# A gated feed-forward and long-convolution kernel: new instruction orders in its opening, and four of its dequantisation units moved

## The reference

```python
xn = layernorm(x)                        # x: 4 x 512 tokens, 512 features, float32
# S4 part: a causal convolution along the feature axis with one kernel K of 512 taps
K = s4_kernel(Lambda, p, q, Vc @ B, Ct, exp(log_step), 512)
y = irfft(rfft(xn, 1024) * rfft(K, 1024))[..., :512] + D * xn
# feed-forward part: weights are 4-bit codes, a 16-entry table (NF4) times one scale per 64 values
Wg, Wu = dequant(gate_q, gate_absmax), dequant(up_q, up_absmax)    # 1792 x 512
Wd = dequant(down_q, down_absmax)                                  # 512 x 1792
h = silu(xn @ Wg.T) * (xn @ Wu.T)
out = x + y + h @ Wd.T
```

## Time and profile before

| | |
|---|---|
| median of 3 runs | 459.49 us (458.85 to 459.49) |
| profiled execution | 460.08 us, span 458.3 us |
| TensorE busy | 438.2 us, 96% of the span |
| VectorE busy | 398.4 us, 87% |
| ScalarE busy | 278.8 us, 61% |
| GpSimd busy | 214.6 us, 47% |
| mean granted TensorE clock | 0.996 |

### The profile page before, as it was taken

How to read it: one execution, slowest core, us unless ns; L and a number is a source line. 1 busy time by engine, 2 the same in 40 slices (tenths; PEclk the granted TensorE clock), 3 DMA queues, 4 the chain that set the end, 5 groups by cost and what they waited for, 6 DMA issues and landing times.

```text
span 458.3 us, 7272 instructions
## 1 busy us (share of the span) xinstructions
PE 438.2 (96%) x2560; PEld 248.8 (54%) x2560; DVE 398.4 (87%) x641; ACT 278.8 (61%) x472; POOL 214.6 (47%) x163
## 2 busy tenths in 40 slices
PE   1879999999999999999999999999999999999997
PEld 1534444443444444434444444466544788888886
DVE  5988979969889798999897879879996999999993
ACT  7868594295877759588684787856032542445340
POOL 2777299547456848669646847778100000000000
PEclk9989999999999999999999999999999999999999
DMA  8543636022315415155222233457691021101111
GB/s 291 172 131 139 144 75 182 1 92 71 138 47 183 161 47 200 54 183 191 63 69 65 61 80 101 111 187 249 193 369 60 1 94 47 46 1 48 47 47 46
DMA packets 34168, 51.41 MB, mean 112 GB/s; under 512 B 13076, under 2 KB 14164, under 8 KB 33364
## 3 DMA queue, kind: packets, MB, share of 16 engines
q1 hardware_dynamic: 34132, 50.95, 35.3%
HBM read 38.03 MB, written 10.81 MB: 107 GB/s over the span
## 4 chain that ended last, share of the span: by engine, by line
PE 85%; DVE 6%; ACT 2%; issue 2%; DMA 2%; POOL 1%; SPq 0%; DVEq 0%; ACTq 0%; POOLq 0%
PE bank L2264 33%; PE bank L2391 21%; PE bank L2109 16%; PE bank L2341 8%; PE bank L2331 6%; ACT work L936 1%; DMA h<-in_x 1%; DVE h L1438 1%; DVE work L1313 1%; DMA work<-in_q_gate 1%; DVE w L1323 1%; DVE work L1309 1%; PE bank L2145 0%; DVE h L1412 0%; POOL h L845 0%
## 5 line engine op out<-in xcount | busy, mean ns | idle before, releaser
L936 ACT ACTIVATE work<-work 128x512 f32<-128x512 f32 (+1 forms) x234 | 130.0, 628 | 11.5 <-POOL work L845 7.8
L845 POOL TENSOR_SCALAR work<-work 128x512 f32<-128x512 int32 x39 | 85.9, 2202 | 64.4 <-DVE work L1309 46.1
L2264 PE MATMUL bank<-h 128*128 128x512 f16 x360 | 81.5, 379 | 0.9 <-ACT bank L1029 0.9
L2109 PE MATMUL bank<-xT,w 128*128 128x512 f16 (+1 forms) x300 | 66.2, 377 | 2.3 <-DVE w L1323 1.1
L2264 PEld LDWEIGHTS bank<-h 128*128 128x128 f16 x360 | 34.9, 98 | 44.0 <-ACT bank L1029 2.4
L2391 PE MATMUL bank<-wd,work 128*128 128x256 f16 x504 | 56.2, 273 | 0.0
L2264 PE MATMUL bank<-xT,w 128*128 128x512 f16 x240 | 55.4, 379 | 0.0
L2391 PEld LDWEIGHTS bank<-wd,work 128*128 128x128 f16 (+1 forms) x504 | 49.3, 98 | 6.0
L2109 PEld LDWEIGHTS bank<-xT,w 128*128 128x128 f16 x300 | 29.4, 99 | 36.8 <-DVE w L1323 2.4
L1250 ACT ACTIVATE work<-h 128x896 f16<-128x896 f32 x30 | 27.9, 942 | 28.4 <-DVE h L2017 18.3
L2391 PE MATMUL bank<-h,work 128*128 128x256 f16 x378 | 42.2, 273 | 0.0
(11 more groups left out here) (181 smaller groups left out, 672.0 us busy)
## 6 DMA issues: line engine op xcount, KB each, us to landing
moved<-h SPq DMA_DIRECT2D x6, 1024.0 KB, 4.9
h<-moved SPq DMA_DIRECT2D x4, 1536.0 KB, 15.5
h<-in_x SPq DMA_DIRECT2D x8, 512.0 KB, 5.4
xT<-in_x SPq DMA_DIRECT2D x16, 256.0 KB, 3.5
out<-xT SPq DMA_DIRECT2D x15, 256.0 KB, 2.1
work<-in_q_gate SPq DMA_DIRECT2D x14, 256.0 KB, 3.6
work<-in_q_up SPq DMA_DIRECT2D x14, 256.0 KB, 2.9
work<-in_am_gate SPq DMA_DIRECT2D x28, 128.0 KB, 3.1
```

What stands on the lines that cost most here:

```text
L845: pool.tensor_scalar(chain_room(u, "r"), qs[:, u % 2, :], RIGHT_FROM, RIGHT_FROM, ALU.max, ALU.subtract).then_inc(first_done, 1)
L936: nc.scalar.activation(room, qs[:, u % 2, :] if j == 0 else room, KNEE, scale=scale, bias=bias, alpha=below).then_inc(knee_done, 1)
L2109: mm = nc.tensor.matmul(out_b, weights(k)[:, unit, wl, f, :], xT[:, TPC * c + first:TPC * c + last, xl, f, :], start=(i == 0), stop=(i == ...
L2264: mm = nc.tensor.matmul(out_b, weight(wl, f), token(xl, f), start=(n == 0 and i in (1, 5)), stop=(n == 5), skip_group_check=i not in (1, 5))
```

## The change

- SyncE: x tiles 4 and 5 are loaded behind the scales of unit 0 and the codes of unit 2, tiles 6 and 7 behind the scales of unit 1.
- Norms: ScalarE makes those of tiles 0, 1 and 4 (before: 0), GpSimd those of the others. A norm on ScalarE waits for its own chunk's `rstd`.
- VectorE's opening: `scales` between the `rstd(0, i)`, the steps of unit 0 behind them; `stats(4)` later; units 2 and 3 relative to `rstd(1, i)` in a new order, `weight_lo(2)` ahead of it.
- TensorE's opening: 8 and 4 `warm_up` matmuls instead of 10 and 6; `products(1, (0,))` ahead of `turn(4)`.
- GpSimd: the 14 `v_step` move behind `first_pass(8)`.
- In window 3 VectorE makes `weight_lo` of unit 9 ahead of both steps of unit 10 (`LO_SOONER`).
- From window 6 on, the `h_mul(n)` behind two slots of dequantisation comes behind one.
- `EARLY_IN` is (7, 9, 11, 12). Window 8 has places 20 and 21, window 12 places 30, 31 and 32, and `LINE_AT` is 31; places from 33 on are as before.

```diff
@@
-EARLY_IN = (7, 8, 9, 11)
+EARLY_IN = (7, 9, 11, 12)
 EARLY = len(EARLY_IN)
@@
         SUMMED = (1,)
-        POOL_NORMS = 1
+        ACT_NORMS = (0, 1, 4)
+        LO_SOONER = made_before(3) + 1
+        def pool_norms(t):
+            return t + 1 - sum(1 for i in ACT_NORMS if i <= t)
         ACC = 4
@@
 sp.dma_start(amf, am_flat).then_inc(amf_ld, 16)
-load_x(2)
-load_x(3)
 load_absmax(0, am_gate[0])
 load_codes(2, q_gate[1])
+load_x(2)
 load_absmax(1, am_up[0])
+load_x(3)
 load_codes(3, q_up[1])
@@
 first_pass(1)
-for t in range(POOL_NORMS, TPC):
-    norm(t)
+norm(2)
+norm(3)
 first_pass(2)
...
 first_pass(4)
-for t in range(TPC, 2 * TPC):
-    norm(t)
+norm(5)
+norm(6)
+norm(7)
 first_pass(5)
-for i in range(14):
-    v_step(i)
 first_pass(6)
@@
 first_pass(8)
+for i in range(14):
+    v_step(i)
 for i in range(EXP_STEPS):
@@
         if s == 0:
-            act.wait_ge(xp_done, NT - POOL_NORMS)
+            act.wait_ge(xp_done, pool_norms(NT - 1))
         else:
@@
 def norm(t):
-    act.wait_ge(rs_step, RSTD)
+    act.wait_ge(rs_step, RSTD * (t // TPC + 1))
     nc.scalar.activation(xnb[:, t % 8, :], xs[:, t, :], ACT.Identity, scale=rs[:, 4, t:t + 1],
@@
     else:
-        act.wait_ge(xp_done, t - POOL_NORMS + 1)
+        act.wait_ge(xp_done, pool_norms(t))
         src, dst = xnb[:, t % 8, :], xst[:, t % 8, HI, :]
@@
 norm(0)
+norm(1)
 chain(1, 5, 6)
+chain(2, 0, 1)
+weight_hi(0)
 x_hi(0)
-weight_hi(0)
 x_hi(1)
-chain(2, 0, 1)
 x_hi(2)
@@
 weight_hi(2)
-chain(3, 2, 4)
+chain(3, 2, 6)
+norm(4)
+silu(0)
+act.wait_ge(b_mm, 1)
+nc.scalar.activation(yv[:, 0:2], bank[3][:, 0:2], ACT.Copy).then_inc(b_cp, 1)
+weight_hi(3)
 x_hi(4)
-chain(3, 4, 6)
-silu(0)
-chain(4, 0, 1)
-weight_hi(3)
+chain(4, 0, 2)
 x_hi(5)
 x_hi(6)
-act.wait_ge(b_mm, 1)
-nc.scalar.activation(yv[:, 0:2], bank[3][:, 0:2], ACT.Copy).then_inc(b_cp, 1)
 x_hi(7)
-chain(4, 1, 6)
+chain(4, 2, 6)
+silu(1)
 h_hi(0)
-silu(1)
+chain(5, 0, 3)
 weight_hi(4)
-chain(5, 0, 6)
+chain(5, 3, 6)
 h_hi(1)
+x_hi(8)
 silu(2)
-x_hi(8)
 weight_hi(5)
@@
         if u in CHAINED:
-            i = (3, 4, 2)[i]
+            i = ((2, 3, 4) if u == LO_SOONER else (3, 4, 2))[i]
         if i != 2:
@@
     elif s == 1 and i == 2:
-        dve.wait_ge(xp_done, NT - POOL_NORMS)
+        dve.wait_ge(xp_done, pool_norms(NT - 1))
     elif s == 1 and i == 0:
@@
 rstd(0, 5)
-step(0, WHOLE)
+scales(1)
 rstd(0, 6)
...
 rstd(0, 8)
-scales(1)
+scales(2)
 rstd(0, 9)
-scales(2)
+scales(3)
 rstd(0, 10)
-scales(3)
+scales(4)
 rstd(0, 11)
-scales(4)
 dve.wait_ge(id_done, 1)
 scales(5)
-stats(4)
 scales(6)
+step(0, WHOLE)
 step(0, SCALED)
-step(1, WHOLE)
 scales(7)
 scales(8)
+step(1, WHOLE)
+weight_lo(0)
 x_lo(0)
-weight_lo(0)
 x_lo(1)
...
 weight_lo(1)
+stats(4)
 stats(5)
 stats(6)
+step(2, WHOLE)
+step(2, SCALED)
 stats(7)
 moments(4, 8)
+weight_lo(2)
 rstd(1, 0)
...
 rstd(1, 3)
+scales(10)
 rstd(1, 4)
+scales(11)
 rstd(1, 5)
-step(2, WHOLE)
+scales(12)
 rstd(1, 6)
...
 rstd(1, 8)
-step(2, SCALED)
+step(3, WHOLE)
 rstd(1, 9)
...
 rstd(1, 11)
-weight_lo(2)
+step(3, SCALED)
+h_mul(0)
+weight_lo(3)
 stats(8)
 x_lo(4)
-scales(10)
-step(3, WHOLE)
-scales(11)
-step(3, SCALED)
-h_mul(0)
-scales(12)
-weight_lo(3)
+stats(9)
 x_lo(5)
 x_lo(6)
-stats(9)
 x_lo(7)
@@
 h_lo(1)
+x_lo(8)
 stats(12)
-x_lo(8)
-stats(13)
 weight_lo(5)
...
 x_lo(11)
+stats(13)
 h_mul(2)
@@
         h_mul(n + 2)
-        stage_of(0, 2)
+        stage_of(0, 1)
         h_mul(n)
-        stage_of(2, 4)
+        stage_of(1, 4)
         join(0, k, 0)
@@
-    if t < POOL_NORMS:
-        pe.wait_ge(xn_done, t + 1)
-    else:
-        pe.wait_ge(xp_done, t - POOL_NORMS + 1)
+    if t in ACT_NORMS:
+        pe.wait_ge(xn_done, ACT_NORMS.index(t) + 1)
+    else:
+        pe.wait_ge(xp_done, pool_norms(t))
     if t >= TPC:
...
-warm_up(10)
-turn(0)
+warm_up(8)
 pe.wait_ge(one_done, 1)
...
 nc.tensor.matmul(bank[0][:, P:P + 6], ones[:], dg3, start=True, stop=True).then_inc(mx_bc, 1)
+turn(0)
 turn(1)
...
 turn(3)
-warm_up(6)
+warm_up(4)
@@
 mm.then_inc(b_mm, 1)
+products(1, (0,))
 turn(4)
-products(1, (0,))
 turn(5)
...
 turn(7)
```

## The result

| | before | changed |
|---|---|---|
| median | 459.17 us (4 runs, 458.57 to 459.49) | 467.13 us (4 runs, 466.05 to 468.28) |
| ratio to before | | 1.0175 [1.0147, 1.0203] |
| profiled execution, span | 460.08, 458.3 us | 466.05, 464.3 us |
| TensorE, VectorE, ScalarE, GpSimd busy | 438.2, 398.4, 278.8, 214.6 us | 438.4, 398.2, 281.8, 220.5 us |

The account below looks back on a forecast made before the run. TensorE, busy 438 of 458 us, bounds the kernel; only its waits or slow stretches pay. 460.08 - 1.5 - 1.2 - 1.2 + 3.9 + 1.6 = 461.7, or 461.1 us against the median; range 455.6 to 463.2.

Parts of the forecast that it names:

- v_step ... so it costs nothing; without that cover it would cost its 3.2 us.: GpSimd's 14 v_step, moved to 61 us, end before gate_copy(8), which waited 5.57 us: cost 0, uncovered 3.2 us.
- h_mul one slot earlier at no cost in the other windows: Windows 10 and 11, where h_mul comes one slot earlier: forecast cost 0.
- window 8, -1.2: TensorE's two waits in window 8, 2.3 us: the first goes, 1.0 stays; gain 1.2 us, bounds 0.9 and 2.3.
- the first joint: Window 8, TensorE's 1.11 us wait before 189.84: goes, as only step WHOLE's 0.7 us or nothing stays ahead of h_mul.
- the second: Window 8, TensorE's 1.19 us wait before 196.22 for the join of side 1: 1.0 of the window's 2.3 us stays.
- the unit in window 12, +3.9: Start of window 13: unit 33's codes stand behind SP's line-write wait, TensorE's join product late; cost 3.9 us, bounds 2.5 and 4.6.
- the forecast's 280.4: Window 12 on ScalarE: block_hi(13, 0) comes at 280.4 us, where it was at 274.38.
- the clock, +1.6: TensorE's clock falls to the 1.2 GHz level behind the 3.9 us gap at window 13: cost 1.6 us, bounds 0 and 2.
- The rival of a fall over the turns of tiles 4 to 7: Opening: the clock falls there too, products(1,(1,)) take 1.7 us more, total 461.8 to 462.8; chance 0.13.
- opening and low half: Chunk 1 starts 1.5 us sooner (0.95 to 2.15); window 4's wait for unit 9's low half shrinks 1.2 us (0.9 to 1.22).
- the first product was to come 0.1 to 0.4 us sooner: Opening: tiles 2 and 3 come some 1.8 us sooner, so TensorE's first product comes 0.1 to 0.4 us sooner.

Follow-up runs that it names:

- run 7: The kernel before with only v_step moved from behind first_pass(5) to behind first_pass(8) on GpSimd: 462.82 us, ratio 1.0073.
- run 9: The kernel before with v_step moved and VectorE's 128x1024 token sums and differences done in two halves: 461.42 us, ratio 1.0028.
- run 10: The kernel before with only VectorE's 128x1024 token sums and differences done in two halves: 461.06 us, ratio 1.0026.
- version 4: The changed kernel with EARLY_IN, v_step and h_mul's slots all put back, new opening and unit 9's sooner low half kept: 457.39 us, ratio 0.9952.
- run 6: The kernel before with only h_mul one slot earlier in every back phase: 461.65 us, ratio 1.0045.
- Run 8: version 4 with EARLY_IN (7, 9, 11, 12), SyncE's wait split, and h_mul early in window 12 alone: 456.82 us, ratio 0.9942.
- Run 5: The changed kernel with SyncE's wait for the Toeplitz line's write, and the table's load behind it, two places later: 462.34 us, ratio 1.0068.
- run 2: The changed kernel with the 14 v_step back behind first_pass(5) on GpSimd: 463.90 us, ratio 1.0088.
- run 1: The changed kernel with EARLY_IN back at (7, 8, 9, 11): 461.57 us, ratio 1.0041.
- run 3: The changed kernel with h_mul(n) back behind two slots: 464.10 us, ratio 1.0088.
- run 11: The kernel before with only unit 9's low half sooner: 459.22 us, ratio 0.9985.

## Why the prediction was wrong

The prediction said 461.1 us, 1.6 slower, and 455.6 to 463.2 at the outside; 467.13 were measured. It put two of the moves at nothing, and these cost 2.9 and 1.9 us; it put window 8 at 1.2 us won, and 0.3 was. With these three put right the sum would have been 7.3. The small differences of the other rows and the clock, which did not fall in the profiled execution, bring it to the 6.1 of the table.

**Failed: "v_step ... so it costs nothing; without that cover it would cost its 3.2 us."** Both halves of the sentence were wrong, and this is the largest miss (+2.9 in the trace, 3.4 alone in run 7). The cover: I took the wait of 5.57 us at gate_copy(8), but between 61 and 92 us the same queue also makes the high half of unit 7 (line 863, in the kernel before 858). From it VectorE makes the low half, for which TensorE waits, and the product that reads both was due at 90.11. Slack at the end of a queue isn't slack of what stands in its middle. The price: I sized the 14 steps by their place in the opening. Rows of the changed kernel's GpSimd:

```profile
61.74 0.66 POOL L799 COPY yv<-yv 128x1 f32<-128x1 f32 x1
...
65.97 0.83 POOL L810 TENSOR_SCALAR V<-yv,cols 128x2 f32<-128x2 f32 x1
66.78 0.82 POOL L813 TENSOR_SCALAR yv<-yv,cols 128x2 f32<-128x2 f32 x1
67.68 1.03 POOL L764 TENSOR_SCALAR sc<-sc 128x1 f32<-128x1 f32 x1
...
86.52 1.94 POOL L850 TENSOR_SCALAR work<-work 128x512 f32<-128x512 int32 x1
88.55 1.58 POOL L863 TENSOR_SCALAR w<-work,sc 128x512 f16<-128x512 f32 x1
```

They run from 61.25 to 67.6: 6.4 us instead of 3.2. The exp steps behind them, pushed deeper into VectorE's long sums, take 18.8 (67.68 to 86.4) instead of 13.4, so the high half comes at 88.55, 9.1 us later than before (79.48), for 3.2 us of moved work. Runs 9 and 10 show that the length of VectorE's instructions sets this, as far as their 0.8 us of uncertainty goes. A rule for it is in the Trainium skill ("SBUF — State Buffer", Who interferes with whom): a VectorE instruction with two inputs in SBUF contends with a GpSimd instruction that reads SBUF, and the one that comes second is blocked for all of the other. The trace agrees, with 2.40 us against 0.27, though the 2.40 span two such instructions. In the opening the steps had been nearly free: in version 4 they fill GpSimd's time from 31.95 to 35.1, a stretch in which the changed kernel's GpSimd waits for codes (4.20 us in all).

**Failed: h_mul one slot earlier at no cost in the other windows.** +1.9 in windows 10 and 11 of the trace, 2.1 in all alone (run 6). I costed what the earlier `h_mul` frees, and of what it delays only the quarter turns, "0.66 us" as an upper bound, never VectorE's own wait for the product that `h_mul` reads. Window 10's loss is that wait. In window 11 the turned rows reach VectorE later as well: VectorE waits 3.01 us for GpSimd at 251.83, 1.48 before.

**Mis-sized: window 8, -1.2.** -0.3 for windows 7 and 8. Run 8 shows the parts: the unit's leaving alone takes 2.3 us of waits to 1.15, just the 1.2 forecast, but with the earlier `h_mul` 1.9 us of waits are left, so it gives 0.7 of that back. I counted its help at the first joint, which run 8 does not need, and nothing against the second.

**Right: the unit in window 12, +3.9.** 3.7 measured, by the mechanism named: SyncE asks for the codes 14.1 us behind the line's write, ScalarE waits 3.14 us and GpSimd 5.04 for them, `block_hi` comes at 282.31, the join behind it. Window 13 starts 2.15 us later than in the kernel before, so this is the forecast's 280.4 to within 0.3. Run 5 moves only the wait, with the table's load behind it, and the gap shrinks to 0.8. That the write took as long as in the one trace read for the forecast is partly luck: over the runs it was 11.0 to 14.0.

**Half right: the clock, +1.6.** Shown in run 2 (1.6 us). It fits the mean clock of the changed kernel's other three executions, 0.993 to 0.996, and that of all 23 executions of runs 1, 4, 5 and 8, which have the new opening and no large gap in window 13: 1.000 in 22 and 0.999 in one. In run 3, with a gap of 1.9 us in its profile, three of six are at 0.996. A mean does not say where the clock fell. But the profiled execution kept 1.00 through a gap of 3.7 us, while run 2's fell behind one of 3.1. What decides, no run here tells. The rival of a fall over the turns of tiles 4 to 7 did not happen: PEclk of the changed kernel where TensorE turned those tiles,

```profile
25.00:28.00 3.00, 2.53 (x12) 0.96 (x10) 2.89 (x17) 1.74 (x3) 0.42 (x1) 1.00 0.45 150
28.00:31.00 3.00, 2.46 (x17) 1.81 (x18) 2.15 (x4) 2.97 (x7) 2.92 (x4) 1.00 0.40 88
31.00:34.00 3.00, 2.67 (x12) 0.99 (x11) 3.00 (x6) 2.97 (x7) 1.55 (x1) 1.00 0.97 358
```
with 16 transposes from 28.38 to 30.9 and no product between 27.4 and 30.9. The other six profiles with the new opening have 1.00 there too, so the rule cited for that rival was not borne out in this stretch.

**Right: opening and low half.** -1.2 of 1.5 and -1.2 of 1.2. Version 4 shows them as a real gain, 2.2 us together (1.4 to 2.9), and run 11 the low half alone as 0.7 (0.1 to 1.3). How closely the opening's size was met stays open, between 1.2 (the one pair), 1.5 (version 4 less run 11) and 2.0 (the means of the profiles); so near a hit is partly luck. Its start was misjudged: the first product was to come 0.1 to 0.4 us sooner and came 0.55 later in this pair (17.68 against 17.13). The prediction saw the fall of the clock there but has no term for its going away.

The parts alone, -2.2, +3.4, +2.1 and, by run 1, +6.2, add to 9.5 where 8.0 were measured: they share window 8, and the gap of window 13 depends on the others (1.9 us in run 3, 3.1 in run 2).

## What to carry to other kernels

When work moves within an in-order queue, find the first reader of each thing behind its new place, not the next long wait of that queue. Price small chained GpSimd steps by what VectorE runs beside them at the new place: duration times count holds only if VectorE's instructions there are as short. A wait on a DMA inside the issuing queue should stand as late as the data's reader allows: moving one such wait by two places gave back 4.9 us by the medians, 2.8 between the profiled executions.

## What the hardware showed

- A chained GpSimd step on 128x1 took 0.19 us with VectorE idle and some 1.27 on average (11.47 for nine) in a stretch of mostly VectorE sums of 128x1024 with both inputs in SBUF, 0.87 (7.79 for nine) with those in halves.
- Between SyncE's issue of the Toeplitz line's write and the next issue, which waits for it, there were 13.1 to 14.0 us in the kernels before and changed and in runs 1, 4, 6, 7, 9 and 11, and 11.0 to 11.5 in runs 2, 3 and 10. The issue itself takes 0.3.
- A gap of some 3 us with little work was followed by the 1.2 GHz level in one execution (run 2) and not in another of nearly the same kernel (the changed one); it cost 1.6 us where the trace shows it. In the old opening such a fall came in four profiles of six.
